# Attention stage of a sandwich layer: probability transposes in two row tiles beside the scores, slot ordered by array mode

## The reference, cut to what matters

```python
q = (x @ Wq).reshape(B, S, H, dk)            # H = 16 heads of 64
k = (x @ Wk).reshape(B, S, H, dk)
v = (x @ Wv).reshape(B, S, H, dv)
scores = jnp.einsum('bqhd,bkhd->bhqk', q / math.sqrt(dk), k)
scores = scores + jnp.where(causal, 0.0, -jnp.inf)
attn = jax.nn.softmax(scores, axis=-1)
out = jnp.einsum('bhqk,bkhd->bqhd', attn, v).reshape(B, S, H * dv)
return x + out @ Wo                           # x is layer-normed before
```

## Time and profile before

| | us |
|---|---|
| median of 3 runs | 1597.46 (1597.28 to 1597.79) |
| the profiled execution | 1598.28 |
| its span on the core | 1596.1 |
| attention, from its first scores to the first matmul of the second feed-forward | 759.86 |
| one sequence in the middle of the attention | 92.44 |
| one slot without extra steps | 11.36 |
| PE busy, share of the span | 97% |
| DVE, ACT, POOL busy | 73%, 49%, 21% |

### The profile page before, as it was taken

One profiled execution on the slowest core, in us unless ns is written; L12 is line 12 of the kernel. 1 busy time (PEld: TensorE's weight loads), 2 busy tenths in 40 slices (PEclk: granted clock), 3 DMA queues, 4 the chain that ended last, 5 costly groups with the idle time before them and its releaser, 6 DMA issues.

```text
span 1596.1 us, 29240 instructions
## 1 busy us (share of the span) xinstructions
PE 1543.7 (97%) x8704; PEld 1041.6 (65%) x8704; DVE 1157.9 (73%) x2733; ACT 777.1 (49%) x1855; POOL 330.9 (21%) x780
## 2 busy tenths in 40 slices
PE   2999999999989999999999999999989999999998
PEld 2666666666666666666666666666656666666665
DVE  6977787777767676776767676776668777877775
ACT  3344333342466656666666656666643443333422
POOL 2000000000144444444444444444320000000000
PEclk9999999999999999999999999999999999999999
DMA  6443333333200000000000000000003333333332
GB/s 188 134 153 102 113 102 104 114 108 114 67 1 2 1 1 1 0 0 0 0 0 0 0 0 0 0 0 1 1 20 115 116 105 117 114 112 117 105 121 86
DMA packets 58801, 97.15 MB, mean 61 GB/s; under 512 B 6144, under 2 KB 15360, under 8 KB 58752
## 3 DMA queue, kind: packets, MB, share of 16 engines
q1 hardware_dynamic: 58752, 96.53, 18.9%
HBM read 92.83 MB, written 3.67 MB: 60 GB/s over the span
## 4 chain that ended last, share of the span: by engine, by line
PE 47%; issue 29%; POOL 19%; DVE 3%; DMA 1%; POOLq 1%; ACT 0%; SPq 0%; DVEq 0%
PE banks L376 17%; POOL work L1272 16%; PE banks L200 9%; PE banks L202 9%; PE banks L201 9%; POOL pool_pace L1267 3%; PE banks L338 1%; PE banks L348 1%; DVE work L1061 1%; DVE work L1033 1%; POOLq L1266 0%; DMA bias<-in_gate_bias 0%; DVE bn L871 0%; DMA work<-cw_rows 0%; PE banks L519 0%
## 5 line engine op out<-in xcount | busy, mean ns | idle before, releaser
L693 ACT ACTIVATE work<-banks 128x512 f32<-128x512 f32 x336 | 200.7, 598 | 463.5 <-PE banks L202 444.1
L1033 DVE TENSOR_TENSOR work<-banks,work 128x512 f32<-128x512 f32 x336 | 231.7, 690 | 155.5 <-ACT work L693 150.6
L376 PE MATMUL banks<-work,wd 128*128 128x512 f32 x672 | 342.9, 593 | 0.3 <-DVE work L1061 0.3
L750 ACT ACTIVATE work<-banks,nmax 128x512 f32<-128x512 f32 (+3 forms) x512 | 263.9, 530 | 31.2 <-DVE nmax L1115 31.2
L1272 POOL TENSOR_SCALAR work<-work,rrec 128x512 f32<-128x512 f32 (+3 forms) x512 | 270.6, 542 | 1.6
L200 PE MATMUL banks<-xT_hi,wg_hi 128*128 (+1 forms) x336 | 248.3, 739 | 0.0
L1061 DVE TENSOR_TENSOR work<-work 128x512 f32<-128x512 f32 x320 | 224.3, 701 | 15.1 <-DVE work L1033 9.5
L1115 DVE TENSOR_REDUCE nmax<-banks 128x2 f32<-128x1024 f32 (+3 forms) x256 | 204.2, 819 | 15.1 <-PE banks L479 13.8
L1133 DVE COPY stage<-banks 128x512 f32<-128x512 f32 x256 | 175.3, 685 | 47.6 <-PE banks L490 47.5
L490 PE MATMUL banks<-small,work 128*128 128x128 f32 x1280 | 199.8, 279 | 7.0 <-POOL work L1272 6.0
L490 PEld LDWEIGHTS banks<-small,work 128*128 128x128 f32 x1280 | 147.8, 141 | 44.3 <-issue 17.3
(11 more groups left out here) (116 smaller groups left out, 2230.2 us busy)
## 6 DMA issues: line engine op xcount, KB each, us to landing
work<-cw_rows SPq DMA_DIRECT2D x320, 256.0 KB, 3.1
x<-in_x SPq DMA_DIRECT2D x8, 256.0 KB, 7.9
out_rows<-x SPq DMA_DIRECT2D x8, 256.0 KB, 2.4
cw_rows<-cwT SPq DMA_DIRECT2D x16, 96.0 KB, 1.9
stage<-in_w_gate SPq DMA_DIRECT2D x3, 448.0 KB, 5.7
stage<-in_w_up SPq DMA_DIRECT2D x3, 448.0 KB, 6.5
wd<-in_w_down SPq DMA_DIRECT2D x3, 448.0 KB, 8.3
small<-in_small SPq DMA_DIRECT2D x1, 576.0 KB, 4.2
```

The lines of the kernel that those rows point to most:

```text
L376: pe.matmul(psY, wd[:, j * P:(j + 1) * P], z[part_slot(j)], start=j == 0, stop=j == HT - 1, skip_group_check=True).then_inc(s["down_ps"], 1)
L693: nc.scalar.activation(silu[j % 2], psG[j % 3], ACT.Silu) \
L750: m = nc.scalar.activation(prob[:, p % 2, i, o:o + w], ps[:, i, so:so + w], ACT.Exp, bias=nmax[:, p % 2, i, qb:qb + 1], accum_out=rsum[:, ...
L1033: tt(gated[j % 3], psU[j % 3], silu[j % 2], ALU.mult) \
```

## The change

Five things are changed, all in the attention.

1. **Transposes as row tiles.** Each 128 x 128 block of probabilities is transposed as two halves of 64 rows (`probT`): the partitions 0 to 63 by one row tile into bank `psT[:, 0]`, the partitions 64 to 127 by the other into `psT[:, 1]`. The stationary operand is 64 rows x 128 columns, the moving one 64 columns of the identity. There are 40 transposes of 64 columns for a pair instead of 20 of 128.
2. **Three groups instead of five parts.** The groups have 8, 8 and 4 blocks and all use the same two banks `psT`. DVE copies groups 0 and 1 (128 x 1024 elements each), ACT copies group 2 (128 x 512).
3. **A slot of four stretches.** Row tiles: scores u=0, transposes 1 of the pair before, scores u=1, transposes 2 of the pair before. Whole array: project k, values, project out, project q. Row tiles: scores u=2, transposes 0. Column tiles: attend of the pair before. The waits for PSUM and for POOL stand ahead of the last two mask products of each score part (`transposes_ready`).
4. **Values of eight heads in one product.** `project_values` now makes one block of 128 tokens x 512 value columns by `mm3`; eight such products make a sequence's values, one per slot, three slots ahead. `Wv` is split in hi and lo like the others, `xT_whole` and its copy are gone, and a second buffer for values is added.
5. **Fewer small steps.** One reciprocal per pair instead of four (`row_rec`), one wait and pace step on POOL instead of four (`norm`), one count of `exp_done` for each score part. The extra steps of a sequence move by a slot (the input's transposes from p=5 to p=4, ahead of project k).

The diff, cut to its core:

```diff
+PT_GROUPS = [PT_BLOCKS[0:8], PT_BLOCKS[8:16], PT_BLOCKS[16:20]]
+        values = [work[:, 10 * CH:].rearrange("p (t d) -> p t d", t=TB),
+                  sb("values", [P, TB, CH])[:, :, :]]
-        psA, psB, psC, psO = bank[4:8]
-        psPT = [psB, psC, psB, psA, psC]
+        psT, psA, psO = pairs[2], bank[6], bank[7]
+            def project_values(parity, k, ps):
+                t, i = k % TB, k // TB
+                rows = slice(parity * CH + t * P, parity * CH + (t + 1) * P)
+                mm3(pe, ps, [x[:, rows] for x in xT_parts],
+                    [w[:, 2, i * CH:(i + 1) * CH] for w in aw], True, True).then_inc(s["v_ps"], 1)
...
                 for k in (0, 1):
+                    if k == 1 and transposes_ready is not None:
+                        transposes_ready()
                     for i in (0, 1):
...
+            def probT(b, p, g):
+                for k, (i, kb, q) in enumerate(PT_GROUPS[g]):
+                    o = q * (q + 1) // 2 * P + kb * P
+                    for h in (0, 1):
+                        r = slice(h * DK, (h + 1) * DK)
+                        m = pe.transpose(psT[:, h, k * DK:(k + 1) * DK], prob[r, p % 2, i, o:o + P],
+                                         ident[r, h * DK:(h + 1) * DK])
+                m.then_inc(s["pT_ps"], 1)
...
+                def second_ready():
+                    if not (first and p == 0):
+                        pe.wait_ge(s["norm_done"], 8 * n)
+                        pe.wait_ge(s["pT_dve"], 2 * n - 1)
+                def third_ready():
+                    if not (first and p == 0):
+                        pe.wait_ge(s["pT_dve"], 2 * n)
+                    scores(*ahead(b, p, 1), 0, False, second_ready)
+                    probT(*ahead(b, p, -1), 1)
+                    scores(*ahead(b, p, 1), 1, False, third_ready)
+                    probT(*ahead(b, p, -1), 2)
+                    pe.wait_ge(s["ctx_sb"], n - 1)
+                if p == 4 and not last:
+                    a_prep(b + 1, psA)
+                if have_q and not special:
+                    project(b2, p2, 1, psA)
+                    project_values((parity + (p >= 5)) % 2, (p + 3) % HP, psT[:, 0, :])
+                    project_out(bo, po, first)
...
                 if have_q:
                     pe.wait_ge(s["k_lo"], n + 3)
+                    project(b2, p2, 0, psA)
+                    scores(*ahead(b, p, 1), 2, False, first_ready)
+                probT(b, p, 0)
+                if not (first and p == 0):
+                    if have_q:
+                        pe.wait_ge(s["q_lo"], n + 3)
                     attend(*ahead(b, p, -1))
```

More of the change, by code:

```diff
@@ new lines, in attn_slot @@
+                if have_s:
+                    scores(*ahead(b, p, 1), 1, False, third_ready)
+                else:
+                    third_ready()
+                if not (first and p == 0):
+                    probT(*ahead(b, p, -1), 2)
+                if first and p == 0:
+                    pe.wait_ge(s["v_sb"], 3)
+                elif first and p == 1:
+                    pe.wait_ge(s["q_lo"], 3)
+                else:
+                    pe.wait_ge(s["ctx_sb"], n - 1)
+                if p == 4 and not last:
+                    a_prep(b + 1, psA)
+                elif p == 4:
+                    pe.wait_ge(s["xn_ready"], NC + 1)
+                    to_columns(psA, xn).then_inc(s["xT_ps"], 1)
+                elif p == 5 and last:
+                    logits(NC, psA, xT)
@@ L539, in attn_slot @@
+                if have_q and not special:
                     if p2 == 0:
                         pe.wait_ge(s["a_xT_lo"], b2 + 1)
-                    project(b2, p2, 0, psA)
-                if first and p == 0:
-                    pe.wait_ge(s["k_lo"], 2)
-                elif first and p == 1:
-                    wait_pT(2, 0)
-                else:
-                    pe.wait_ge(s["ctx_sb"], n - 1)
-                probT(b, p, 0)
-                if have_s:
-                    scores(*ahead(b, p, 1), 1, False)
@@ L560, in attn_slot @@
                     project_out(bo, po, first)
[L561 to L570 removed]
+                if have_q and special:
+                    if p == 4 and not last:
+                        pe.wait_ge(s["a_xT_lo"], b + 2)
+                    elif p == 4:
+                        pe.wait_ge(s["xT_hi"], NC + 1)
+                    else:
+                        pe.wait_ge(s["sigmoid_done"], NC + 1)
+                    project(b2, p2, 1, psA)
@@ L1101, in part_lo @@
                 hi, lo = [t[:, p % 2, :] for t in qk[which]]
-                ps = psA if which == 0 or not early else psB
+                ps = psT[:, 1 - which, :] if early else psA
                 if which == 0:
@@ L1147, in attn_slot @@
                 if not (first and p < 1):
-                    pT_copy(*ahead(b, p, -1), 4, first and p < 3)
-                row_rec(b, p, 3)
+                    pT_copy(*ahead(b, p, -1), 1, first and p < 3)
+                row_rec(b, p)
                 if p == 2 and not first:
@@ L1170, in attn_slot @@
                     rows_mean(b - 1, b - 1 + 2 * NC)
-                if p in (2, 3) and not last:
-                    a_rows(b + 1, False, (2 * (p - 2), 2 * (p - 2) + 1))
-                if p == 4 and not last:
+                if have_q:
+                    part_lo(*ahead(b, p, 2), 0, False)
+                pT_copy(b, p, 0, first and p < 2)
+                if p in (1, 2) and not last:
+                    a_rows(b + 1, False, (2 * (p - 1), 2 * (p - 1) + 1))
+                if p == 3 and not last:
                     a_residual(b + 1)
@@ L1186, in attn_slot @@
                     normalise(0, "xn_ready")
-                if p == 4 and last:
-                    xT_low(NC)
                 if last and p >= 6:
@@ L1255, in _ @@
             pool.wait_ge(s["consts_loaded"], 48)
-            for w in range(2):
+            for w in range(3):
                 pool.wait_ge(s["aw_hi"], w + 1)
```

303 lines of the change are left out of this document (128 added, 175 removed).

## The result

The change makes the kernel 0.4% faster: 1591.21 us (1588.39 to 1593.26) against 1597.56 (1597.28 to 1597.79), ratio 0.9957, interval 0.9942 to 0.9972. The forecast was 1574: right in sign, and the time lies inside the forecast's 1555 to 1592, but at its far edge: 6.3 us came where 23.5 were expected. One execution of a later kernel (1880.27 us, at a granted clock of 0.75 throughout) is left out of that kernel's times.

What follows compares the result with a forecast made beforehand. PE's list bounds the kernel before, a ring of waits after: 8 x 10.63 + 4.5 = 89.5 us a sequence, -2.9. Eight give -23.5: 1598.3 to 1574.8, median 0.8 lower, 1574; forecast 1555 to 1592, 8-in-10 range 1546 to 1632.

Steps and rivals of the forecast that it cites:

- PE's own work, 9.51: PE's work in a plain attention slot: 11.36 us less 0.72 for form changes, 0.94 for transposes, 0.19 for values.
- The rival that transposes don't get cheaper: A pair of transposes costs 0.107 us or more, and the kernel is 58 longer, 1632 us; chance 0.15.
- The reason given against that rival: Rows of the earlier trace show transposes' loads starting 60 ns apart, against the skill's 107 ns for 128 columns.
- DVE's copy, 1.23: DVE's copy of a group of transposes, 1024 elements in a row, takes 1.23 us, upper bound 1.37.
- The ring, 10.63 a slot: Plain slot's chain: copy of transposes 1, transposes 2, k, q and their parts, attend, scores u=0, transposes 1; 10.63 us.
- The wait at copy 1: PE waits 0.4 to 1 us for DVE's copy of transposes 1, between the mask products of scores u=1.
- q waiting 1.6 for k's low part in p=4: In slot p=4, q waits 1.6 us for k's low part, since both use the one bank psA.
- Eight of them: -23.5: A sequence of the attention takes 89.5 us against 92.44, -2.9; eight sequences give -23.5 us.
- zero, with 4 either way: First slot without a previous pair's transposes set against the last pair's bare hand-overs: zero, 4 us either way.
- two hand-overs of the last pair: At the attention's end, the last pair's two more hand-overs now stand bare: 1.9 and some 1.2 us.
- Feed-forward stages: Outside the attention, zero change; the prediction is wrong if the two feed-forward stages move by more than 2 us.
- The clock falls: Rival: after PE's waits the granted clock is 0.65 in all slots, 5 us a slot, some 1900; chance 0.02.

Runs made afterwards that it cites:

- experiment 3: On the changed kernel with PE's loop written out: DVE's list alone reordered, 1574.07 us; k alone moved with ACT's matching copy, 1593.68; both together, 1540.01.
- experiment 1: The changed kernel with PE's loop written out, 1582.21 us; the kernel before with PE's loop as three turns of two sequences, 1601.3.
- the two other kernels with the old slot: The kernel before with PE's loop as three turns of two sequences, 1601.3 us; the kernel before with one square root replaced by a copy, 1598.23.
- The fastest kernel: The changed kernel with PE's loop written out, DVE's list reordered and k moved between transposes 1 and scores u=1, 1540.01 us.
- `unrolled_ends`: The changed kernel with PE's loop written out and DVE's single steps at both ends moved, 1583.36 us; same moves on The fastest kernel, 1541.97.

## Right and wrong, by the prediction's own steps

- **PE's own work, 9.51: right.** 0.06 a pair of transposes; three products of values, 0.76 to the start of what follows them (756.07 to 756.83) against 0.71 forecast and 0.90 before; 9.90 in a PE-bound slot with two more changes of form. The rival that transposes don't get cheaper is out: the trace has a pair each 60 ns, with a load of 128 columns for each of its two tiles. So the rule it rested on (the Trainium skill, TensorE: Matmul & The Clock Gate, section LDWEIGHTS: by columns alone, an estimated 107 ns for 128) doesn't hold for these row tiles.
- **The reason given against that rival: wrong, and lucky.** The prediction took from the earlier trace rows that the loads of whole transposes start 60 ns apart. That holds for the first two of a group alone. The same view with the window's end moved on has the third done 0.31 after the first began and the fourth 0.42, so they start 110 ns apart, as the transposes do, and that agrees with the rule. What 16 loads cost in row tiles, no row of before could say; it is the last row, after the change:

```profile
720.29 0.31 PEld L490 LDWEIGHTS banks<-small,work 128*128 128x128 f32 x3 [0.17 <-issue]
...
720.29 0.42 PEld L490 LDWEIGHTS banks<-small,work 128*128 128x128 f32 x4 [0.17 <-issue]
...
695.88 0.57 PEld L489 LDWEIGHTS banks<-small,work 64*128 64x128 f32 x16
```

- **DVE's copy, 1.23: right**, 1224 ns.

```profile
L1158 DVE COPY stage<-banks 128x1024 f32<-128x1024 f32 x71 | 86.9, 1224 | 74.5 <-PE banks L489 74.5
```

- **The ring, 10.63 a slot: right in size and place.** 10.64 measured, and a sequence 89.24 against 89.5. The wait at copy 1 is 0.31, not 0.4 to 1, because a wait of 0.15 for a second chain (copy 0, row maxima and exponentials u=2), which the prediction didn't follow, stands ahead of it. With that one gone the wait at copy 1 is 0.68 to 0.76 and the slot the same (experiment 3).
- **q waiting 1.6 for k's low part in p=4: right.** It is 1.50 in the middle (679.50) and 1.41 in the last sequence.
- **"Eight of them: -23.5": wrong.** This is the step that failed. -2.9 was taken from a middle sequence and given to the first and the last one too, with "zero, with 4 either way" for the ends. The first has +1.0 and the last +4.1 where -2.9 stood: 3.9 and 7.0 us, 10.9 of the 17 that are missing. The prediction saw two hand-overs of the last pair and named 1.9 and 1.2; the tail is 2.3 longer. Not seen were p=4 (19.13 for 17.50) and p=5 (16.01 for 12.67). There the second stage's transposed input, then its logits, go through psA ahead of k, and k ahead of q; before, input and logits had another bank (psC) and transposes beside them. How much of the 7.0 that is, and how much the square root and the clock, no run shows. PE's waits in these two slots, in us, times and the longest:

```profile
PE banks L478 <- DVE stage L1158: 4.5, 2, 4.2
PE banks L196 <- DVE k_lo L1136: 4.4, 2, 3.0
```

- **PE's loop: not in the prediction at all.** It read the diff's loop as what it computes, not as a body twice as long: 6.7 us in the profile (91.43 + 89.48 + 93.57 less three times 89.25), 9.0 in the medians of experiment 1 (1591.21 and 1582.21).
- **Feed-forward stages: not the change's.** The first is 1.5 longer, from its first weights on (POOL's first split starts at 18.33 for 16.70); but over all traces the attention starts at 434.8 to 436.7, whichever the slot, so that is spread. The second is 0.5 shorter (400.75; 400.89 in the two other kernels with the old slot). Both are under the 2 us set as the limit. One thing was changed here after all, though "The change" doesn't list it: the table `iota` is shorter and is read by a broadcast. The step that reads it takes 948 ns in both.
- **The clock falls: right in kind.** The forecast case of 0.65 in all slots didn't come, but stretches of that kind did, at the ends and behind the second branch, and they are part of what these cost. That the clock would fall more often there is what "I put these against each other, zero" leaves out:

```profile
1126.11:1130.32 4.21, 0.01 (x2) 0.00 (x0) 3.37 (x12) 1.10 (x3) 0.00 (x0) 0.92 0.00 0
1130.32:1134.50 4.18, 4.18 (x20) 3.08 (x20) 2.73 (x4) 2.96 (x4) 3.99 (x8) 0.50 0.02 4
...
897.28:900.55 3.27, 0.00 (x1) 0.01 (x1) 0.00 (x0) 2.10 (x9) 0.00 (x0) 1.00 0.00 0
900.55:905.00 4.45, 4.24 (x45) 3.15 (x46) 1.92 (x3) 0.12 (x1) 0.46 (x2) 0.62 0.02 4
```

In the earlier trace rows it was 3.47 standing and then 0.65. Before, the attention has three slots below full, p=0 of the first sequence (0.83), p=4 of the last (0.90) and the tail (0.93). After, there are also the stretch ahead of p=0 (0.94), p=1 and p=2 of the first (0.87), the slot behind the second branch (0.85) and p=5 of the last (0.89), and p=4 is at 0.82. But the stand of 1.99 at the first branch left it full.

The sum: 23.5 forecast, less 10.9 for the ends, less 6.7 for the loop, less 1.5 for the start, and back 1.4 for the middle sequences' better size and 0.5 for the second feed-forward, is 6.3.

## What to carry to other kernels

A gain read from the steady middle holds for the middle alone: lay out a first and a last round apart, with what each queues behind, once the bound has moved from an engine's list to a ring of hand-overs. When waits take the place of an engine's work, list all rings through that engine and their lengths before changing one, and again with the change made: the one that opens the longest can lengthen the next, as 10.64, 10.65 and then 9.90 show. Read a rate from the steady part of a group, not from its first two. And count the instructions of a loop body in a diff, not only its rounds.

## What was not expected of the hardware

- A branch back over a body of two sequences (about 1430 of PE's matmuls in the old slot, 1670 in the new one, and as many loads) costs 1.4 to 3.3 us here; over one sequence, as before, nothing is to be seen at any branch, nor anywhere in the straight code of six sequences.
- The same work can be followed by either clock. Two sequences of the kernel with k alone moved (experiment 3) have the same stretch of slot p=4, busy 6.19 of 9.14; in one the clock stays full behind it, in the other it is 0.65, and that slot takes 15.17 instead of 13.66:

```profile
672.00:681.14 9.14, 6.19 (x62) 3.90 (x58) 5.56 (x8) 5.82 (x17) 4.29 (x9) 1.00 0.01 2
681.14:686.00 4.86, 4.86 (x53) 3.08 (x53) 2.85 (x4) 1.75 (x6) 0.00 (x0) 1.00 0.00 0
762.00:771.14 9.14, 6.19 (x62) 3.90 (x58) 5.56 (x8) 5.82 (x17) 4.29 (x9) 1.00 0.00 0
771.14:776.00 4.86, 4.86 (x39) 3.43 (x41) 1.39 (x2) 1.72 (x5) 0.00 (x0) 0.65 0.02 3
```

The fastest kernel has one such slot among its six in the middle (14.54 for 13.02), and three with the moves of `unrolled_ends`, 3.0 us more in that profile, which is more than the two medians differ by (1540.01 and 1541.97). What decides between the two stays open here.
- Two row tiles load their operands side by side: 128 columns on each every 61 ns, where whole loads come every 109 ns.
